# Keys and values of all tokens first, queries projected between the score steps

## The reference, cut to what matters

```
x: [8, 256, 512]                                    # 2048 tokens in fp32, 8 sequences (batches)
q, k, v = x Wq^T, x Wk^T, x Wv^T                    # 8 query heads, 4 key/value heads of 64
q, k = rope(rms(q) * (1 + gq)), rope(rms(k) * (1 + gk))   # rms over each head of 64
k_blocks, v_blocks: new k, v written at the sequence's positions (paged cache, block table)
att = softmax(q k^T / 16, causal, window of 256) v  # keys gathered through the table
a   = att Wo^T
M_e = W0 + scatter(softmax(eaw) @ atoms * sigmoid(imp))_e  # one 512 x 512 table for each of 8 experts, 4096 cells changed
x   = x + top-2 mixture of a M_e^T                  # layer 0
x   = x + top-2 mixture of gelu(h fc1_e + b1) fc2_e + b2,  h = x W1^T + LoRA   # layer 1
```

## Time and profile before

| | |
|---|---|
| median of 3 runs | 1101.1 us (1100.79 to 1107.58) |
| profiled execution: own time, span | 1111.89 us, 1110.1 us |
| busy over the span | PE 948.5 (85%), DVE 558.0 (50%), ACT 404.3 (36%), POOL 299.2 (27%) |
| mean granted PE clock | 0.927 of full speed |
| first and last start of the score reduction L1404 | 181.3 and 458.2 us |
| first transpose of layer 0 on PE | 493.5 us |

### The profile page before, as it was taken

How to read it: one execution, slowest core, us unless ns; L and a number is a source line. 1 busy time by engine, 2 the same in 40 slices (tenths; PEclk the granted TensorE clock), 3 DMA queues, 4 the chain that set the end, 5 groups by cost and what they waited for, 6 DMA issues and landing times.

```text
span 1110.1 us, 17908 instructions
## 1 busy us (share of the span) xinstructions
PE 948.5 (85%) x4626; PEld 622.4 (56%) x4627; DVE 558.0 (50%) x2233; ACT 404.3 (36%) x1205; POOL 299.2 (27%) x248
## 2 busy tenths in 40 slices
PE   5999968998796887719889988899199999999994
PEld 2464466665463554414444437778177777777772
DVE  5768784676575887632334432354323333333331
ACT  3424314775563554301111111122154444455540
POOL 3000104345674241112334430223212221221221
PEclk9989957999897998959999997989599999999998
DMA  8665552445534353158777746983733334333430
GB/s 272 230 229 194 190 178 60 133 118 152 166 89 124 126 174 104 52 173 246 203 198 127 131 71 219 358 274 135 226 98 62 55 66 74 68 64 69 74 47 0
DMA packets 82532, 156.27 MB, mean 141 GB/s; under 512 B 16135, under 2 KB 29111, under 8 KB 80880
## 3 DMA queue, kind: packets, MB, share of 16 engines
q1 hardware_dynamic: 38272, 84.87, 23.5%
q0 software_dynamic: 25520, 45.11, 19.8%
q10 hardware_dynamic: 18688, 25.71, 7.4%
HBM read 94.05 MB, written 73.19 MB: 151 GB/s over the span
## 4 chain that ended last, share of the span: by engine, by line
PE 49%; DVE 16%; DMA 15%; issue 9%; POOL 4%; DVEq 3%; SPq 1%; ACT 1%; ACTq 0%; POOLq 0%
PE ps L618 39%; DMA m_buf<-tot,cell_i 6%; DMA acc<-R,tok_i 5%; PE ps L624 3%; PE ps L710 2%; DVE R L1323 1%; DMA R<-acc 1%; DVE R L1437 1%; DVE R L1315 1%; DMA rows<-zrow 1%; DVE R L1333 1%; POOL m_buf L532 1%; PE ps L667 1%; DVE R L1415 1%; PE ps L698 1%
## 5 line engine op out<-in xcount | busy, mean ns | idle before, releaser
L618 PE MATMUL ps<-R 128*128 128x128 f32 (+4 forms) x2768 | 681.0, 403 | 18.5 <-DMA R<-in_x_t 11.4
L618 PEld LDWEIGHTS ps<-R 128*128 128x128 f32 x2768 | 421.2, 194 | 245.9 <-issue 227.2
L590 POOL DMA_INDIRECT out_x<-R,tok_i x39 | 60.7, 1556 | 252.5 <-DVEq L1754 164.4
L624 PE MATMUL ps<-ident,R 128*128 128x128 f32 x440 | 67.3, 286 | 58.4 <-DMA R<-rows 48.1
L963 ACT ACTIVATE R<-R,nmx 128x384 f32<-128x384 f32 x128 | 77.5, 607 | 94.0 <-DVE nmx L1404 85.6
L524 POOL DMA_INDIRECT rows<-R,slot_i x64 | 65.6, 1025 | 156.6 <-DVEq L1511 76.6
L624 PEld LDWEIGHTS ps<-ident,R 128*128 128x128 f32 x440 | 54.0, 147 | 90.7 <-issue 75.5
L590 POOL DMA_INDIRECT acc<-R,tok_i x39 | 60.8, 1558 | 123.1 <-DVE R L1663 114.9
L698 PE MATMUL ps<-ident,R 128*128 128x128 f32 x384 | 57.1, 285 | 40.4 <-DVE R L1415 34.9
L1112 ACT ACT_TABLE_LOAD x18 | 23.1, 1283 | 147.9 <-PE ps L618 147.9
L1104 ACT ACTIVATE R<-R 128x2048 f32 x39 | 75.6, 1940 | 1.8 <-issue 1.8
(11 more groups left out here) (281 smaller groups left out, 892.3 us busy)
## 6 DMA issues: line engine op xcount, KB each, us to landing
R<-rows SPq DMA_DIRECT2D x78, 258.0 KB, 3.3
R<-in_fc ACTq DMA_DIRECT2D x16, 1024.0 KB, 5.6
m_buf<-R SPq DMA_DIRECT2D x8, 1024.0 KB, 5.2
R<-m_buf SPq DMA_DIRECT2D x16, 512.0 KB
R<-acc SPq DMA_DIRECT2D x32, 256.0 KB
new_kv<-R SPq DMA_DIRECT2D x16, 256.0 KB, 2.0
qn<-R SPq DMA_DIRECT2D x16, 256.0 KB, 2.3
R<-qn SPq DMA_DIRECT2D x8, 512.0 KB
```

What stands on the lines that cost most here:

```text
L590: po.indirect_dma_start(out=sums[s], out_offset=bass.IndirectOffsetOnAxis(ap=tok_i[:, s:s + 1], axis=0), in_=y_sb[s], in_offset=None, boun ...
L618: m = pe.matmul(out, lhs(k), rhs(k), start=(k == 0 and first), stop=(k == KC - 1 and last))
L624: m = pe.transpose(out[:, k * P:(k + 1) * P], src[:, k * P:(k + 1) * P], ident[:])
```

## The change

The first stage makes only keys and values: one bank for a tile, eight banks in turn, the scaling of the keys on ACT (`scaled`), four output buffers, no `qn`. Query tile t is projected into bank 0 (`project_q`, uses `p0` and `p1`); ACT squares its 8 heads (`squares_q`), DVE applies rope straight from the bank (`rope_q`) and leaves it unscaled in `q_in`; POOL works out the 16 reciprocal roots of a batch by Newton steps (`scales`), and `tops` takes them as the factor of its reduction, after a wait on `q_nw` at each period's start. Tiles 0 and 1 are projected between the first stage and period 0, tiles 2B+2 and 2B+3 in steps 2 and 4 of period B. The gate fold comes after the last key tile, then the second query tile, then `delta` (64 matmuls of 64 rows and 64 columns). The comparison tables, the cell sums and `move_cells` go into period 0, and two thirds of the index work into periods 0 and 1 (batches 0 and 1 before attention, 2 to 4 and 5 to 7 in four pieces each). `a0`, `a1` are copied out by ACT. POOL's cells come 8 in each pass; half of the zeroing of `m_buf` is moved behind the start of attention. In the last three periods one cell addition is made in a step, from step 3 of period 5 on, which are 21 of 32; the 11 others follow `tiles()` after attention.

```diff
+        USES = {"open": ("p0", "p1", "q0", "k0", "k1"),
+                "first": ("q1", "p0", "p1", "ct", "q0", "k0", "k1"),
+                "mid": ("a0", "q1", "h0", "p0", "a1", "p1", "h1", "q0", "k0", "k1", "rt"),
+                "last": ("a0", "q1", "h0", "a1", "h1", "rt", "a2"),
                 "after": ("h2", "rt")}
...
+            for b in range(NB):
+                if b + 1 < NB:
+                    sp.wait_ge(S["bk"], uses(b - 1)["p1"] + 1)
+                    for t in range(2):
+                        load_q(2 * b + 2 + t)
...
+                for m in range(2, 6) if b == 5 else range(6, 10) if b == 6 else ():
+                    sp.wait_ge(S["m_done"], m - 1)
+                    fetch_m(m)
-            for m in range(6, 16):
+            for m in range(10, 16):
                 sp.wait_ge(S["m_done"], m - 1)
                 fetch_m(m)
...
+            def scales(b):
+
+                po.wait_ge(S["q_ss"], 2 * b + 2)
+                po.tensor_scalar(nw_x[:], ssq[:], 1.0 / HD, RMS_EPS, ALU.mult, ALU.add)
+                po.drain()
+                po.tensor_scalar(nw_y[:].bitcast(I32), nw_x[:].bitcast(I32), -0.5, 1597463007.0, ALU.mult, ALU.add)
+                po.drain()
+                for n in range(3):
+                    po.tensor_tensor(nw_t[:], nw_y[:], nw_y[:], ALU.mult)
+                    po.drain()
...
+                po.tensor_scalar(q_scale[:, b % 2, :], nw_y[:], -SCALE, None, ALU.mult)
+                po.drain().then_inc(S["q_nw"], 1)
...
                     if add:
                         cells(t + 2 + n)
+                if b + 1 < NB:
+                    scales(b + 1)
                 if add:
                     cells(t + 6)
+                    cells(t + 7)
...
+            def project_q(at, t):
+
+                pe.wait_ge(S2["xq"][t % 2], 16 * (t // 2) + 16)
+                wait(pe, bc, at[f"p{t % 2}"])
+                chunks(ps[:, 0, :], lambda k: xq[t % 2][:, k, :], lambda k: wq[:, k, :]).then_inc(bk, 1)
...
+            pe.wait_ge(S["kv_nr"], NT - 7)
+            project_q(opening, 0)
...
+            project_q(opening, 1)
+            pe.wait_ge(S["pre_c"], 1)
...
+            for t in range(ST):
+                for x in range(2):
+                    m = pe.matmul(ps[64 * x:64 * x + 64, 6 + x, t * NE:(t + 1) * NE], at_v[64 * x:64 * x + 64, t, :],
+                                  eaw_t[64 * x:64 * x + 64, :], start=True, stop=True)
+            m.then_inc(S["delta"], 1)
+            turn_q(opening, 0)
...
+            def scaled(t):
+                x = t % 2
+                ac.wait_ge(S["rst"], t + 1)
+                wait(ac, S["p1r"], t - 1)
+                for h in range(NG):
+                    ac.activation(nrm[x][:, h * HD:(h + 1) * HD], ps[:, t % 8, h * HD:(h + 1) * HD], ACT.Copy, scale=rstd[:, x, h:h + 1])
...
+            def squares_q(at, t):
+
+                wait(ac, S["q_nw"], t // 2)
+                wait(ac, bk, at[f"p{t % 2}"] + 1)
+                for h in range(NH):
+                    c = ac.activation(sq_q[t % 2][:, h * HD:(h + 1) * HD], ps[:, 0, h * HD:(h + 1) * HD], ACT.Square,
+                                      accum_out=ssq[:, t % 2 * NH + h:t % 2 * NH + h + 1])
+                c.then_inc(S["q_ss"], 1)
...
+            def rope_q(t):
+
+                ve.wait_ge(S["q_ss"], t + 1)
+                rope(ps[:, 0, :], rq_a, rq_b, tabq_a, tabq_b, NH, t).then_inc(S["bc"], 1)
...
             def tops(B, j):
 
+                if j == 0:
+                    ve.wait_ge(S["q_nw"], B + 1)
+                    ve.memset(junk_a[:, 0:1], 0.0)
                 wait(ve, S["s_dot"], 16 * B + 2 * j + 2)
...
+                    tops(B, j)
+                    if j == 0:
+                        build_mask(1)
+                    if j == 2 and not last:
+                        outside(B + 1)
+                    if j in (1, 2) and first:
+                        sparse_eq(4 * j - 4, 4 * j)
                     if j == 3 and not last:
+                        rope_q(2 * B + 2)
+                    if j == 5 and not last:
+                        rope_q(2 * B + 3)
+                    if j == 5 and not last:
                         build_mask(0)
+                    if B < 2 and j in (3, 4, 5, 6):
+                        next(index)
+                    if j == 6 and first:
+                        move_cells()
...
+                    if B == 5 and j >= 3 or B > 5:
+                        next(adds, None)
...
+            rope_q(0)
             outside(0)
             build_mask(0)
-            move_cells()
+            rope_q(1)
+            cell_weights()
             periods(ve, period)
```

More of the change, by code:

```diff
@@ L997, in period @@
                     if j == 6 and not last:
+                        q_out(at, 0, 1 - s)
+                    if j == 7 and not last:
                         k_out(at, 0, 1 - s)
-                    if j == 7 and not last:
                         k_out(at, 1, 1 - s)
```

641 lines of the change are left out of this document (326 added, 315 removed).

## The result

The changed kernel takes 1144.0 us (median of 4 runs, 1140.1 to 1149.9) against 1103.6 for the kernel before on the same chip: ratio 1.037, 95% interval 1.030 to 1.044. Forecast were 1090, in a range that ended at 1115, so the miss is 54 us. The profiled execution is 1140.7, its span 1138.9, 28.8 over the span before.

A forecast was written before the change was run, and what follows sets the result against it. No single engine bounds the whole; PE bounds plain middle periods, DVE's additions hinder periods 5 and 6. Opening -63, attention +42 and tail +10 sum to -11: 1101.1 to 1090 us, range 1066 to 1115.

The forecast's parts named there:

- period 6: Attention period 6: keeps 8 table additions, saves 3.1 us on DVE and gets 4 of rope: 41 us.
- the sum for a middle period: Periods 2 to 4: 30.3 us before, 6.9 more PE work, 1.3 for rope and bank 0 waits: 38.5 each.
- the opening: Stretch to the first reduction: 118 us against 181.3, -63, with bounds of 106 and 128.
- the wait for POOL: Heads of periods: `q_nw` late by 1 to 2 us for two periods, 3 us counted in periods 2 to 4.
- period 0: First attention period: 24.4 us plus 25.1 of added work step by step, 49.5 in all, +24.7.
- index pieces in period 1: Period 1: four index pieces for three batches, 9 us on DVE where PE is long anyway: 40.5 instead of 38.5.
- additions in period 5: Period 5: keeps 5 of 11 table additions at 1.03 us each and loses a 7.9 us wait: 39 us.
- the tail: After period 7: 11 additions left over, SP's zeroing queued behind the last fetch: +10 us, bounds 7 and 12.
- the pair of key tiles at 6.0 us: Opening: exchange of ACT and DVE for each pair of key tiles, 6.0 us; six pairs make 36.
- The step with the cell sums: Period 0, step 5: cell sums hold PE 6.9 us at full clock ahead of the scores of step 6: +7.3.
- the third rival: POOL sets the pace: waits on `q_nw` heading periods 2 to 5, scales 12 us, +25, time 1115; chance 13%.
- The second and third rivals: The second: opening and bank 0 chain longer, first reduction at 128, period 0 at 54, time 1104; chance 20%.

The follow-up runs named there:

- e4: Changed kernel with query weights, first query tiles, atoms and raw output weights loaded from the fourth to the eighth key tile on: 1144.8 us, ratio 1.036.
- e8: Changed kernel with comparisons, cell sums and their copying moved back ahead of the periods: 1135.2 us, ratio 1.027.
- e13: Changed kernel without the periods' query work (8-column product, one square, two small copies remain) and with one table addition of 32: 1095.5 us, ratio 0.991.
- e7: Changed kernel with a quarter of the periods' query product and one table addition of 32: 1115.7 us, ratio 1.011.
- e16: Changed kernel with query loads ahead of tables 4 and 5, cells in the opening, zeroing ahead of the last four fetches, scales before the fourth scatter: 1121.9 us.
- e14: Kernel before, with output product h0 at the end of step 1, ahead of the scores of step 2: ratio 1.006.
- e9: Changed kernel with h0, a1 and h1 behind the scores of steps 2, 4 and 6, query products at the ends of steps 2 and 4: 1155.4 us.
- e6: Changed kernel with one of the 32 indirect additions to the expert table, the other 31 left out: 1136.2 us, ratio 1.027.
- e17: Changed kernel with SP's accumulator and row-end writes of batches 0 to 6 half a period later, behind the next query loads: 1137.7 us, ratio 1.030.
- e11: Changed kernel with SP's zeroing of the region ends issued ahead of the last four table fetches: 1143.1 us, ratio 1.028.
- e3: Changed kernel with the loads of query tiles 14 and 15 ahead of the fetches of tables 4 and 5: 1130.1 us, ratio 1.023.
- e12: Changed kernel with e9, e3 and e11 together, plus comparisons in the opening and cell sums behind period 0's first scores: 1140.0 us, ratio 1.026.

## Why the prediction was wrong, by its own steps

By size, in us of the 40 that the traces show: the queue in period 6, which the sum had at nothing, 14.4; the sum for a middle period 8.0, that is 1.6 in each of periods 1 to 5; the opening 6.3; the wait for POOL, with what else periods 2 to 4 have over a clean one, 5.5 beyond the 3 that were counted; period 0 4.6; index pieces in period 1 and additions in period 5 3.2 and 2.4; period 7 and the tail gave 4.4 back.

**The opening: right in kind, 6 us short.** PE does idle ahead of `project_q(1)`. The tile took 6.5 us and `delta` 7.2, together 13.7 for the 15.5 forecast. The miss lies ahead of them, in `project_q(1)` starting at 103.4 and not at 96. The step is the pair of key tiles at 6.0 us: the DVE timeline has the reciprocals of three pairs at 64.84, 71.84 and 79.28, 7.0 and 7.4 apart, and PE waited 13.4 us for an x tile before that, which my sum did not have. e4 shows that issuing the bulk loads later does not help, since the waits moved with them; whether the volume of the loads or the exchange of ACT and DVE sets the 7 us was not separated.

**Period 0: 49.5 forecast, 54.1 measured.** The step with the cell sums was mis-sized: 6.9 us "at full clock", but the sums took 10.5, and steps 5 and 6 together 24.1 for 19.3 (6.1 with +7.3 and +5.9). e8 shows what the cells cost there, 17.7 us, but also that they cost 12.6 in the opening, so putting them into period 0 lost 5.1 us by the traces.

**Middle periods: two terms wrong, in opposite directions.** The step that failed is the sum 30.3 + 6.9 + 1.3 = 38.5, in which the output products and their copies cost nothing though their place changes. The runs split a clean period thus: 30.2 before; 34.6 with the new order and no query work (e13, +4.4); 36.1 with a quarter product, squares and ropes (e7, +1.5); 40.1 with all of it (e16, +4.0). So the query work cost 5.5, less than my 8.2, and what the new order leaves without it, which I had at nothing, cost 4.4. That 38.5 lay only 1.6 under the clean 40.1 is luck. I had named only the wait for bank 0 behind a query product. That the 4.4 come from the place of h0 and h1 is argued from the steps that grew. e14 and e9 show that h0's place alone is a small part in the kernel before, and that undoing the order is worse while both products share a bank; which of the copy on ACT, the turn behind it, the 8-column products in bank 0, h1 and a1 make up the rest was not tried one by one. Period 1 has 5.2 us over a clean one, 3.5 of it in step 6, where I had 2 for the index pieces; period 5 has 2.8, in steps with table additions.

**POOL: the third rival, by another price.** I expected 3 us from late scales in two periods. Beyond the clean 40.1, periods 2 and 3 have 3.3 and 4.7 us, period 3's in a cold step 1 (8.7 for 5.8) and in step 3 (7.6 for 5.7). The rival had the place (`q_nw` at the head) right and its price wrong: an operation with its drain is 0.36 and not 0.8, 5 us in all and near my 4.8 (which should have read 4.5, fifteen at 0.3), but the drain behind an indirect transfer adds 2 to 9. From scales to scales POOL takes 45.7, 44.9 and 42.8 us, where I had 40 for a pass. e6 takes the long drain away, e17 shortens it, and their medians are 6 to 8 us lower; both intervals overlap that of the changed kernel, and e11, with short drains, wins nothing in these periods. So how much of the time is POOL's is not settled. The rule of the Trainium skill that I put beside this rival (page "SBUF — State Buffer", section "Who interferes with whom") would show as longer steps. The 13 from 215.76 to 220.53 take 0.37 each. In the pass ahead of period 7 the trace agrees with the rule: three of POOL's operations last until a DVE operation with two SBUF inputs ends, 0.62, 0.52 and 0.93 us for some 0.2. Two of them, and the DVE operations beside them:
```profile
435.77 0.62 POOL L536 TENSOR_TENSOR nw_t<-nw_y 128x16 f32<-128x16 f32 x1
437.21 0.93 POOL L540 TENSOR_SCALAR nw_t<-nw_t 128x16 f32<-128x16 f32 x1 [0.16 <-issue]
```
```profile
435.62 0.69 DVE L1421 TENSOR_TENSOR R<-R 128x512 f32<-128x512 f32 x1
437.05 1.08 DVE L1537 TENSOR_TENSOR R<-R 128x512 f32<-128x512 f32 x1
```
It costs 1.4 us in that pass and less than 0.5 in those ahead of periods 2 to 5, a small part of what the rival lacked. The same section of the Trainium skill lays a stalled transfer of GpSimd's to DVE holding the shared port. Here DVE's work was the same in e17, and moving SP's writes alone shortened the drain from 7.15 to 1.73: what held it was other transfers.

**Period 6: a queue passed over.** 41 forecast, 55.4 measured, 11 of it gone with e3. I counted the fetches of the tables and the query loads, each by itself, and not that the loads of period 6 are queued behind fetches that wait for period 6's own additions.

**The tail: the mechanism was in part right, the bounds were not.** To the first turned rows it is 52.4 us for 35.8 before, +16.6 where I had 7 to 12. The zeroing behind the fetches, which I had named as the cause, covers only 3 of it (e11); behind it lie the additions that are left over, with DVE as what ends last. Then 8 us came back where I expected none: two windows that cover the linear stage have 42.5 and 45.0 us before, 40.8 and 39.0 after, and the second was granted 0.92 before and 1.00 after. Ahead of the fall of the clock stands a wait: PE stops 5.31 us at 723.74 for a choice of experts by DVE, which itself had idled 3.45 for a load of accumulator rows. After the change PE waits 1.06 us in that place, at 755.51, and e14, which is the kernel before but for one product, waits 5.76 as the kernel before does. Why the load comes earlier was not traced. Layer 0 gives 2 more (169.0 and 166.7). Sum +6.4.
```profile
705.00:750.00 45.00, 39.69 (x211) 34.10 (x210) 19.64 (x131) 9.45 (x30) 12.07 (x12) 0.92 0.90 325
...
723.74 0.20 PE L833 MATMUL ps<-selb,tri 128*128 128x16 bf16 x1 [5.31 <-DVE selb L1474]
```
```profile
740.00:779.00 39.00, 37.94 (x214) 33.02 (x213) 20.03 (x133) 9.86 (x31) 12.38 (x12) 1.00 1.02 379
```
The first fence has that second window of the kernel before and the wait in it, the second fence the window of the changed one.

**The chances.** The second and third rivals had been kept apart; parts of both came true at once, and with period 6 the sum left the range. Adding up: opening +6.3, period 0 +4.6, periods 1 to 4 +15.1, periods 5 and 6 +18.4, period 7 and tail -4.4, together 40.

**What stays open.** e6 has periods of 41.7 where e16 has 40.1, with no wait on POOL; the excess is in steps 3 and 4 (6.8 and 5.7 for 5.7 and 5.1), as it is in e11. It stands between PE and those who wait for it. In e6 the scores that step 4 needs are recorded as ended at 285.03, and the reduction starts only at 286.19 (e16: 277.76 and 277.85):
```profile
284.11 0.92 PE L703 MATMUL ps<-R 64*128 64x384 f32 x4
286.19 0.61 DVE L1508 CUSTOM_DVE_ANT_0 R<-ps,R,q_scale 128x384 f32<-128x384 f32 x1 [2.01 <-issue]
```
In e11 the gap is 2.1 us (285.97 to 288.12). Since the ends of matmuls are modelled, the trace does not say whether PE ended late or its signal came late.

## What to carry to other kernels

When work is moved into a loop whose bound is one engine in order, write out every instruction of that engine between one product that others wait for and the next: what is newly *ahead* of it can cost its whole length in that step, even if the engine's total is unchanged, and only a trial shows how much later steps give back (2.0 lost and 1.4 given back in e14). For each DMA queue, list the waits of the issues in program order across neighbouring iterations; a load behind a fetch that waits for this iteration's work is a stall of that work. An engine that computes and also issues indirect transfers, as POOL does here, pays for the transfers at its next drain, and what that costs depends on who else is writing then. And a wait that is taken away can come back in another step, so read the whole period and not only the wait.

## What the runs showed of the hardware

A GpSimd drain behind an indirect transfer lasts with the transfers on the DMA engines: 0.7 to 1.2 us in the changed kernel where POOL had issued none for 4 us and more (2.0 in the opening of e12), 1.7 to 2.8 just behind a table addition when SP's writes were elsewhere (e17), 7.33 and 1.64 for the same instructions when SP's writes were issued ahead of the addition or behind it (changed kernel and e11), up to 8.7 (e3, pass of batch 2) with 1 to 2 MB of SP's writes ahead. The small operations themselves (16 elements a partition) take 0.20 to 0.25 us on GpSimd for the most part, 0.36 with a drain, and 0.52 to 0.93 beside a DVE operation with two SBUF inputs (435.77 to 438.14). A stall of PE costs more than itself here: behind the one of 4.85 us step 1 has 8.7 us for 5.8, and the turns, transposes and mixes there took 1.09, 1.49 and 2.83 us for 0.63, 0.82 and 1.52, at a granted clock of 0.54 from 269 to 275, so for most of that stretch at the lower of the two levels, 1.2 GHz.
